# Biases behind each half of the scores, and the units of the row maximum in two places of a step instead of three

## The reference

```python
q = (x @ Wq.T + bq).reshape(b, n, h, hd).transpose(0, 2, 1, 3)
sim = jnp.einsum('bhid,bhjd->bhij', q, k)
bias = rel_emb[rp_bucket]
sim = sim + jnp.transpose(bias, (2, 0, 1)) * SCALE
sim = sim + causal                       # -inf where j > i
attn = jax.nn.softmax(sim, axis=-1)
out = jnp.einsum('bhij,bhjd->bhid', attn, v)
return out @ Wo.T + bo
...
rw = jnp.zeros_like(rw).at[..., 0].set(1.0)
h = jax.nn.relu(jnp.einsum('bsd,edf->besf', tgt, w1) + b1[None, :, None, :])
```

## Time and profile before

| | |
|---|---|
| median of 3 runs | 401.53 us (400.35 to 402.07) |
| profiled execution, its own time | 402.29 us |
| its span, first to last instruction | 400.5 us |
| busy, share of the span | TensorE 80%, VectorE 72%, ScalarE 46%, GpSimd 17% |
| mean granted TensorE clock | 0.924 |
| the 8 groups | from about 78.6 to 365 us |

### The profile page before, as it was taken

How to read it: one execution, slowest core, us unless ns; L and a number is a source line. 1 busy time by engine, 2 the same in 40 slices (tenths; PEclk the granted TensorE clock), 3 DMA queues, 4 the chain that set the end, 5 groups by cost and what they waited for, 6 DMA issues and landing times.

```text
span 400.5 us, 8158 instructions
## 1 busy us (share of the span) xinstructions
PE 321.0 (80%) x3197; PEld 153.1 (38%) x3197; DVE 287.5 (72%) x960; ACT 184.0 (46%) x258; POOL 69.5 (17%) x78
## 2 busy tenths in 40 slices
PE   0182438396999899799889979988988998999982
PEld 0131215143334335334434433443443344337752
DVE  3985356358668589588678848967875996773986
ACT  1042024131655554575565545556555545873330
POOL 9812035700001000100100100010010000161552
PEclk9996586668699999999999989999998999999998
DMA  8013422410012101201201220331222010100011
GB/s 227 26 53 116 145 90 95 148 64 3 2 43 66 39 18 52 81 1 61 75 12 44 68 64 2 86 88 26 65 79 55 15 16 12 33 2 10 5 52 53
DMA packets 18295, 21.97 MB, mean 55 GB/s; under 512 B 5584, under 2 KB 14960, under 8 KB 18256
## 3 DMA queue, kind: packets, MB, share of 16 engines
q1 hardware_dynamic: 18256, 21.45, 18.5%
HBM read 14.98 MB, written 4.23 MB: 48 GB/s over the span
## 4 chain that ended last, share of the span: by engine, by line
PE 51%; DVE 17%; DMA 15%; ACT 7%; issue 5%; SPq 4%; POOL 1%; DVEq 0%; POOLq 0%; ACTq 0%
PE ps L1015 14%; PE ps L1044 13%; PE ps L1001 13%; DMA QA<-mrow 7%; ACT PT L626 6%; PE ps L1032 5%; DMA qk_scratch<-QS 4%; DVE FM L759 3%; DVE XN L701 2%; DVE junk L766 2%; DMA KA<-qk_scratch 2%; DMA rows<-in_vectors 2%; PE ps L1077 2%; DVE st L836 1%; DVE U L889 1%
## 5 line engine op out<-in xcount | busy, mean ns | idle before, releaser
L626 ACT ACTIVATE PT<-ps 128x1024 f32<-128x1024 f32 (+1 forms) x192 | 145.8, 810 | 132.4 <-PE ps L1032 101.9
L759 DVE TENSOR_REDUCE FM<-ps 128x1 f32<-128x512 f32 (+3 forms) x176 | 108.4, 660 | 29.2 <-PE ps L1001 29.1
L1001 PE MATMUL ps<-KA,QA 96*128 96x256 bf16 (+3 forms) x544 | 108.7, 294 | 17.6 <-DMA KA<-qk_scratch 14.3
L1015 PE MATMUL ps<-QA,KA 98*128 98x512 bf16 (+3 forms) x384 | 99.0, 343 | 25.4 <-DMA QA<-mrow 10.3
L766 DVE CUSTOM_DVE_ANT_0 junk<-ps,NB 128x256 bf16<-128x256 f32 (+1 forms) x224 | 78.8, 403 | 37.3 <-PE ps L1001 37.2
L1044 PE MATMUL ps<-PT,VG 128*16 128x512 f32 (+3 forms) x768 | 86.9, 498 | 0.0
L1001 PEld LDWEIGHTS ps<-KA,QA 96*128 96x128 bf16 x544 | 44.1, 101 | 103.7 <-DVE FM L759 32.9
L1015 PEld LDWEIGHTS ps<-QA,KA 98*128 98x128 bf16 x384 | 32.5, 101 | 52.5 <-ACT PT L626 21.6
L497 POOL COPY NB<-NBH 128x1024 bf16<-128x1024 bf16 x7 | 7.3, 1040 | 212.3 <-PE ps L1044 211.4
L1032 PE MATMUL ps<-TT,flb 128*32 128x176 f16 (+4 forms) x1152 | 38.9, 245 | 0.0
L1032 PEld LDWEIGHTS ps<-TT,flb 128*32 128x32 bf16 x1152 | 21.5, 96 | 17.9 <-issue 17.0
(11 more groups left out here) (88 smaller groups left out, 255.5 us busy)
## 6 DMA issues: line engine op xcount, KB each, us to landing
QA<-qk_scratch SPq DMA_DIRECT2D x48, 96.0 KB
KA<-qk_scratch SPq DMA_DIRECT2D x16, 288.0 KB
TT<-f_scratch SPq DMA_DIRECT2D x16, 120.0 KB, 7.8
qk_scratch<-QS SPq DMA_DIRECT2D x4, 384.0 KB
qk_scratch<-QS SPq DMA_DIRECT2D x12, 128.0 KB
X<-in_x SPq DMA_DIRECT2D x2, 512.0 KB, 6.2
out<-U SPq DMA_DIRECT2D x4, 256.0 KB, 2.3
xnT<-OT SPq DMA_DIRECT2D x28, 32.0 KB
```

The costliest lines, as they stand in the source:

```text
L626: nc.scalar.activation(PT[:, s % 3, 2 * q:2 * q + 2, off:off + w], ST[:, q, :, off:off + w], ACT.Exp).then_inc(s_exp, 1)
L759: nc.vector.tensor_reduce(FM[:, ib, heads[0]:heads[-1] + 1, piece], bank[:, 0:w * len(heads)].rearrange("p (h n) -> p h n", n=w), AX.X, AL ...
L1001: last = nc.tensor.matmul(bank[:, i * w + j - j0:i * w + j - j0 + n], QA[0:KS, p, ib // 4, h, (ib % 4) * 128:(ib % 4 + 1) * 128], KA[0:KS, ...
L1015: last = nc.tensor.matmul(ST[:, q, h % 2, off:off + w], KA[0:KST, p, jb // 4, h, (jb % 4) * 128:(jb % 4 + 1) * 128], QA[0:KST, p, ic, h, o ...
```

## The change

In `group`, `biases` takes the half q and is called right behind `scores` of that half, at the same place in the first step ahead of the loop. The units that stood at position 1 pass to position 0 or 2; position 1 is now behind the values too and gets cost 0, so it holds none in the steady groups. The costs and the three shares are new, and so every unit stands elsewhere: unit 37 is now at position 0 of step 11 of the group before (it was at step 0 of its own), unit 38 at position 0 of step 0 (it was at position 2, behind the values), unit 13 at position 0 of step 5 (it was at position 2).

```diff
@@ places
-        half = 2 * step_cols(ic, jb)[1] + (640 if near_cols(ic, jb) else 0)
-        for pos, cost in enumerate((half, half, 4.2 * step_cols(*STEPS[s])[1])):
+        half = 2 * step_cols(ic, jb)[1] + (850 if near_cols(ic, jb) else 0)
+        rest = 4.2 * step_cols(*STEPS[s])[1] + 240
+        for pos, cost in enumerate((half + rest / 2, 0, half + rest / 2)):
-S_START, S_END, M1_AT = 0.15, 1.03, 1.06
+S_START, S_END, M1_AT = 0.09, 0.965, 1.0
@@ TensorE's program
-            def biases(p, s):
+            def biases(p, s, q):
                 ...
-                for q in range(2 if near else 0):
-                    for h in range(2 * q, 2 * q + 2):
+                if not near:
+                    return
+                for h in range(2 * q, 2 * q + 2):
                 ...
@@ group
                     if at:
                         scores(*at, 0)
+                        biases(*at[1:], 0)
                     s_units_at(s, 0)
                     if at:
                         scores(*at, 1)
-                    s_units_at(s, 1)
-                    if at:
-                        biases(*at[1:])
+                        biases(*at[1:], 1)
                     if s == 0:
                         pe.wait_ge(s_vg, g + 1)
                     values(g, p, s)
+                    s_units_at(s, 1)
                     s_units_at(s, 2)
@@ ahead of group 0
             for q in range(2):
                 scores(0, 0, 0, q)
+                biases(0, 0, q)
                 unit(0, 0, OWN0 + q)
-            biases(0, 0)
```

More of the change, by code:

```diff
@@ L1026, in biases @@
                 near = near_cols(ic, jb)
-                for q in range(2 if near else 0):
-                    for h in range(2 * q, 2 * q + 2):
[L1029 to L1035, removed]
+                if not near:
+                    return
+                for h in range(2 * q, 2 * q + 2):
+                    for c, u0, n in near:
+                        for e in range(2):
+                            r0 = 64 * c + 32 * e
+                            last = nc.tensor.matmul(ST[r0:r0 + 32, q, h % 2, off:off + n], flb[:, 32 * e:32 * e + 32],
+                                                    TT[:, p, h, u0:u0 + n], start=False, stop=True,
+                                                    skip_group_check=True)
+                last.then_inc(s_str, 1)
             def values(g, p, s):
```

## The result

The changed kernel takes 406.44 us (median of 10 runs) where the kernel before took 401.07 (10 runs on the same chips). The ratio is 1.0147, with a 95% interval of 1.0105 to 1.0189, so it is slower by about 1.5%. Ratios leave out executions that lay more than 1.5% above the fastest of their kernel, so they are not the quotients of the medians. The profiled execution took 406.01 us with a span of 404.2, so it is 3.7 us over that of before; the medians are 5.4 apart.

What follows compares the result with a forecast made beforehand. TensorE's program bounds the groups, the DMA queue the hand-over's end. Seven rests + 3.9, first and last group + 0.1, clock + 1.3, units 0: + 5.3 us on 402.29, or 406.8 by the median, said as 407; range 400.5 to 412.

Steps and rivals of the forecast that it cites:

- The queue: Hand-over, step 11's last biases to next step 4: unit 38's rows land with the loads ahead; it keeps 12.4 us.
- A pair of gaps at 0.2 us: Each of 9 steps with biases: a second pair of TensorE layout changes costs 0.2 us, 1.8 a group.
- The rest at + 0.55: Group outside the hand-over: five steps' gaps + 1.0 us, less waits won at 205.43 and unit 13; between + 0.2 and + 1.1.
- Full places cost nothing: Two or three units at one place, on three banks: no wait over 0.1 us found, 0 to 0.3 a group.
- No other wait in the hand-over: Hand-over: TensorE's work grows 0.8 us to 10.7, under 12.36, so hidden under the wait for rows, costing nothing.
- The clock: Waits ahead of step 4 grow to about 1.9 to 2.9 us: one more fall, + 1.3 us, ends 0 and + 5.2.
- First and last group together + 0.1: First group + 0.4 us, gaps against a wait gone; last group - 0.3; bounds for both - 1.5 to + 2.
- The sum: Whole kernel: + 5.3 us on the profiled execution's 402.29, giving 407.6; 406.8 against the median, stated as 407.
- Rival A: Hand-over: unit 38's rows come earlier, - 1.55 us in each of six groups, total 393.6 us; chance 0.12.
- Rival D: Unit places: bunches of units stall TensorE through the banks by 1 us a group more, total 414 us; chance 0.05.

Runs made afterwards that it cites:

- e3: Changed kernel with wider loads (queries' and keys' loads with outermost count 8, not 3): 386.66 us, ratio 0.9555 to the kernel before.
- e4: Kernel before with wider loads (queries' and keys' loads with outermost count 8, not 3): 376.12 us, ratio 0.9306 to the kernel before.
- e5: Changed kernel with narrow loads, TT's load issued behind unit 38's rows and not ahead: 400.81 us, ratio 0.9946 to the kernel before.
- e2: Kernel before with its unit places, only the biases split, each half's right behind its scores: 408.85 us, ratio 1.0086.
- e1: Changed kernel with its unit places, but both halves' biases behind the second scores again: 406.83 us, ratio 1.0070 to the kernel before.
- e6: e3 with unit 38 behind the values of step 0 again: 379.23 us, ratio 0.9353 to the kernel before.
- e11: e3 with GpSimd's two copies at a group's end held until VectorE has turned the maxima behind unit 37: 380.59 us, ratio 0.9439.
- e10: Changed kernel with narrow loads, unit 38 behind the values of step 0 again: 415.85 us, ratio 1.0292 to the kernel before.
- e9: Changed kernel once more, unedited, beside e10 on one chip: 407.74 us, ratio 1.0107 to the kernel before.

## Why the prediction was right or wrong

The forecast of 407 us and its direction held (406.44), and so did its main mechanism: a second pair of gaps in each step with biases, paid where nothing hides it. Its parts held less well, and two of them were wrong and in part cancelled.

- *The queue.* Right. Issued 1.6 us sooner behind the loads, the rows let step 4's scores start no sooner: they stay 12.09 us behind the loads in the period shown. e3, e4 and e5 moved the landing by moving what stands ahead in the queue. The Trainium skill (DMA: Bandwidth & Descriptors, Queues, rings and completion order) has one ring for each queue row and engine, which is what six packets behind the loads and two at once look like.
- *A pair of gaps at 0.2 us.* Right: 0.21 from e2, and 0.1 from pieces of biases to a unit in the changed kernel, which no row of before showed. The Trainium skill (TensorEngine Tiling (Array Packing), Key Properties) says that a change of tiling mode drains TensorE; the gap of 0.1 us at each such change in this trace agrees.
- *The rest at + 0.55.* It was + 0.67 in groups 1, 2, 3 and 5. The waits that I had put at 0.45 to win went (0.50 to 0.04 by the starts), so the pairs and unit 13 in its new place cost 1.13 and not 1.0.
- *Full places cost nothing.* Right with the split, and I had the cover right: e1 takes the biases away from between them, and 1.18 us of waits appear. In e1's expectation I forgot this cover myself.
- *No other wait in the hand-over.* Wrong. I added up TensorE's work and did not follow VectorE's turned maxima, which unit 38 needs much sooner now, nor look at what GpSimd does at that time. In the end I find no cost of its own, since the rows' wait took it in; in e3 it costs 0.9 us a group in groups 2 to 6 (e6, e11).
- *The clock.* Wrong in sign. I took waits of 1.9 to 2.9 us ahead of step 4 and one more low stretch. The waits were 0.80 to 1.79 in groups 2 to 6 and none in group 1, because part of the idle time now lies ahead of unit 38, and the profile has one low stretch for two before. With unit 38 late (e10) there are three. My bound by the length of the wait was too simple as well: in e10 waits of 2.41, 2.05 and 2.04 us go with a low stretch, those of 1.86 and 1.78 in groups 2 and 3 do not, nor does one of 1.90 in group 5 of e2, while 1.77 does in group 4 of e9.
- *First and last group together + 0.1.* Measured: + 0.54 and + 0.12 for the first, - 1.30 and + 0.41 for the last, so - 0.2.
- *The sum.* On the profiled executions + 3.7 where I had + 5.3. Against my terms the rests came out 0.6 us higher (the clock left aside) and the hand-overs 0.8, the first and last group 0.3 lower and the clock 2.6 lower. What the 0.8 us in the hand-overs are stays open. That the median still came out at 407 is in part luck: the profiled execution of before lay 1.2 us over the median of these 10 runs, and that of after 0.4 under its own.

Rival A (rows land sooner) is shown false for this change. Its price of 1.55 us a hand-over was about right where the landing was made sooner by other means: 1.59 in e4, where the clock also fell in no group behind the first. Rival D (banks) is shown false with the split and true without it. What stays open is what decides on the clock besides the length of a wait, and how the wider loads win 12 us ahead of the groups.

## What to carry to other kernels

A small DMA that a step waits for lands when what stands ahead of it in its queue has passed: before moving its producer, count the packets of the loads in front and how many pass at a time, and give those loads an outermost count that spreads them. Work added under such a wait is free until someone removes the wait; here it hid 0.61 of the 1.29 us that the change costs a group. Group matmuls by the shape they take in the array (0.1 us for each change here), and split them only at the step where an engine stands waiting.

## What the runs showed of the hardware

- A cast of 128 x 16 on VectorE took 1.03 us in place of 0.17 when it started 0.04 us after a bf16 copy of 1.04 us on GpSimd, and ended with it; a subtraction behind it took 0.31 in place of 0.18 beside GpSimd's next copy. In the kernel before, an addition with a maximum (L766), which reads PSUM, took 0.42 us beside the same copy, as without it. The Trainium skill (SBUF — State Buffer, Who interferes with whom) states that a port pair is shared by the two engines and held by whichever starts first for its whole instruction, and that a VectorE copy or cast, or an operation with two inputs in SBUF, can need it; the trace agrees, and I had not looked for it.
- One piece of idle TensorE time of 2.0 to 2.4 us went with half the clock in groups 4, 5 and 6 of e10, and about the same amount in two pieces in group 4 alone of e9. In groups 5 and 6 of e10 the low stretch lasts 6.8 us, where the two of the kernel before last 3.4: group 5's rest is 24.66 us for 21.66.
- The same 0.9 MB of DMAs in a hand-over passed sooner when the outermost count of the loads was 8 and not 3: the last packet of 4 KB came 6.7 us behind the issue in e4 and 10.3 before, with six to eight such packets at a time for 3.2 us in place of three. The kernel before became 7% faster by this alone.
